# A graph layer on one core: another order for VectorE's instructions in the second round

## The reference

```python
h = jnp.maximum(_layernorm(x, axis=-1), 0.0)
hi_t = h @ W1_w[:HID] + dep_emb @ W1_w[HID:] + W1_b          # dep_emb = dep_emb_table[adj]
hj_t = h @ W2_w[:HID] + dep_emb @ W2_w[HID:] + W2_b
relevance = jnp.sum(hi_t * hj_t, axis=-1)
A = softmax(jnp.where(adj != 0, relevance, NEG), axis=2)
h_syn = relu((A @ h) @ gcn_w + gcn_b)
out = x + h_syn @ Wo_w + Wo_b
```

## Time and profile before

| | |
|---|---|
| median of three runs | 366.44 us (366.13 to 366.99) |
| the profiled execution | 366.79 us, span 364.9 us |
| PE busy | 354.9 us, 97% of the span |
| ACT busy | 272.9 us, 75% |
| DVE busy | 263.1 us, 72% |
| POOL busy | 178.8 us, 49% |
| granted TensorE clock | 1.00 throughout |
| the chain that ended last | PE 91%, DVE 5%, ACT 3%, issue 1% |

### The profile page before, as it was taken

One profiled execution on the slowest core, in us unless ns is written; L12 is line 12 of the kernel. 1 busy time (PEld: TensorE's weight loads), 2 busy tenths in 40 slices (PEclk: granted clock), 3 DMA queues, 4 the chain that ended last, 5 costly groups with the idle time before them and its releaser, 6 DMA issues.

```text
span 364.9 us, 9504 instructions
## 1 busy us (share of the span) xinstructions
PE 354.9 (97%) x3144; PEld 222.5 (61%) x3144; DVE 263.1 (72%) x667; ACT 272.9 (75%) x580; POOL 178.8 (49%) x348
## 2 busy tenths in 40 slices
PE   8999879999999999999999999999999999999986
PEld 8675546565756666565756666565756666565753
DVE  1788898595867777695867777695867777586664
ACT  3499586969698787879788787879788787865742
POOL 2046871573828284654728274654728274680000
PEclk9999999999999999999999999999999999999999
DMA  7962607764649484554649384564649364444052
GB/s 225 362 208 85 175 3 141 220 115 134 176 112 232 86 249 97 178 120 145 160 104 241 86 237 108 163 132 141 167 96 249 86 172 86 116 89 143 2 154 107
DMA packets 82215, 53.87 MB, mean 148 GB/s; under 512 B 45666, under 2 KB 82148, under 8 KB 82196
## 3 DMA queue, kind: packets, MB, share of 16 engines
q1 hardware_dynamic: 81488, 53.22, 55.8%
q0 software_dynamic: 64, 0.20, 0.3%
q10 hardware_dynamic: 644, 0.20, 0.3%
HBM read 17.44 MB, written 12.58 MB: 82 GB/s over the span
## 4 chain that ended last, share of the span: by engine, by line
PE 91%; DVE 5%; ACT 3%; issue 1%; DVEq 0%; POOL 0%; POOLq 0%
PE bank L1135 24%; PE bank L1136 24%; PE bank L1137 24%; PE bank L1233 5%; PE bank L1376 3%; PE bank L1371 3%; PE bank L1179 2%; PE bank L1147 2%; PE bank L1342 1%; PE bank L1170 1%; PE bank L1218 1%; PE bank L1441 1%; PE bank L1443 1%; DVE wo_lo L774 1%; DVE stats L683 1%
## 5 line engine op out<-in xcount | busy, mean ns | idle before, releaser
L422 POOL TENSOR_TENSOR h_parts<-h_tok,h_parts 128x1536 f16<-128x1536 f32 (+1 forms) x14 | 41.9, 2994 | 92.7 <-ACT h_parts L467 92.7
L1135 PE MATMUL bank<-gw_hi,hT 128*128 128x385 f16 x192 | 63.1, 329 | 1.9 <-DVE g_parts L867 1.6
L398 POOL TENSOR_TENSOR x_all<-x_all,bo_all 128x1536 f32 (+1 forms) x16 | 55.1, 3450 | 16.5 <-ACT h_tok L476 16.5
L1137 PE MATMUL bank<-gw_hi,hT 128*128 128x385 f16 x192 | 62.7, 327 | 0.0
L1136 PE MATMUL bank<-gw_lo,hT 128*128 128x385 f16 x192 | 62.6, 326 | 0.0
L1135 PE MATMUL bank<-wo_hi,z_hi 128*128 128x384 f16 x180 | 58.7, 326 | 0.0
L1136 PE MATMUL bank<-wo_lo,z_hi 128*128 128x384 f16 x180 | 58.7, 326 | 0.0
L1137 PE MATMUL bank<-wo_hi,z_lo 128*128 128x384 f16 x180 | 58.7, 326 | 0.0
L1135 PE MATMUL bank<-hT,m_hi 128*128 128x512 f16 x144 | 54.6, 379 | 0.5 <-DVE hT L697 0.5
L1136 PE MATMUL bank<-hT,m_hi 128*128 128x512 f16 x144 | 54.6, 379 | 0.0
L1137 PE MATMUL bank<-hT,m_lo 128*128 128x512 f16 x144 | 54.6, 379 | 0.0
(11 more groups left out here) (162 smaller groups left out, 691.9 us busy)
## 6 DMA issues: line engine op xcount, KB each, us to landing
x_all<-in_x_dram SPq DMA_DIRECT2D x16, 768.0 KB, 6.1
out_dram<-x_all SPq DMA_DIRECT2D x15, 768.0 KB, 4.0
hg_parts<-hg_lo SPq DMA_DIRECT2D x32, 192.0 KB, 3.3
hg_parts<-hg_hi SPq DMA_DIRECT2D x32, 192.0 KB, 3.6
x_all<-in_L_gnn_W_w_dram SPq DMA_DIRECT2D x2, 576.0 KB, 5.0
out_dram<-x_all SPq DMA_DIRECT2D x4, 192.0 KB, 1.9
gcn_raw<-in_L_gnn_gcn_w_dram SPq DMA_DIRECT2D x1, 576.0 KB, 10.8
x_all<-in_L_gnn_Wo_w_dram SPq DMA_DIRECT2D x1, 576.0 KB, 11.3
```

What stands on the lines that cost most here:

```text
L398: nc.gpsimd.tensor_tensor(x_all[:, s, :, :], x_all[:, s, :, :], bo_all[:, :, :].broadcast_to([P, KT, D]), ALU.add).then_inc(x_biased, 1)
L422: nc.gpsimd.tensor_tensor(h_parts[:, tiles, 1, :], h_tok[:, tiles, :], h_parts[:, tiles, 0, :], ALU.subtract).then_inc(h_split, 1)
L1135: nc.tensor.matmul(dst, lh, rh, start=(c == 0), stop=False)
L1137: last = nc.tensor.matmul(dst, ll, rh, start=False, stop=(c == DC - 1))
```

## The change

Three lists move, and no arithmetic changes.

DVE, before the jump of `typed`: the three `wo_low_part` are taken out of `second_round` and put behind the first `type_top`, behind `rows_and_low(0, 2)` and behind `rows_and_low(0, 3)`.

DVE, in `second_round`: `g_low_part(1, 0)` comes straight after `masked_scores(0)`; the statistics of x(3) are cut in two halves; `attention_high(1)` and the second half come ahead of `shared_high_parts(2)`; only the first half of the mask's bias is waited for at the start.

POOL: the second half of the mask's bias is made after `main_coefficients(2)` and no longer before it; `token_low(2)` comes before `main_coefficients(3)`.

```diff
@@ gpsimd
             make_bias(0)
+            main_coefficients(2)
             make_bias(1)
-            main_coefficients(2)
...
+            token_low(2)
             main_coefficients(3)
-            token_low(2)
@@ vector
-            def second_statistics(tiles):
+            def part_statistics(s, tiles):
+                if s == 1:
+                    dve.wait_ge(x1_loaded, 16)
+                    dve.wait_ge(coef_ready, COEF_STEPS)
+                else:
+                    dve.wait_ge(x_loaded, 16 * s)
+                    dve.wait_ge(coef_ready, COEF_STEPS * 2)
                 for k in tiles:
-                    ins = nc.vector.bn_stats(stats6[:, k, :], x_all[:, 1, k, :])
+                    ins = nc.vector.bn_stats(stats6[:, k, :], x_all[:, s, k, :])
...
+            wo_low_part(0)
             rows_and_low(0, 1)
...
             rows_and_low(0, 2)
+            wo_low_part(1)
             rows_and_low(0, DC)
+            wo_low_part(2)
...
             def second_round():
-                early_low_part(1, 0)
-                wo_low_part(0)
-                early_low_part(1, 1)
-                wo_low_part(1)
-                early_low_part(1, 2)
-                dve.wait_ge(bias_made, 2)
+                for c in range(DC):
+                    early_low_part(1, c)
+                dve.wait_ge(bias_made, 1)
                 masked_scores(0)
-                wo_low_part(2)
-                statistics(3)
+                g_low_part(1, 0)
+                part_statistics(3, range(0, 2))
+                attention(0, prev=False)
                 third_mean_made()
-                g_low_part(1, 0)
-                attention(0, prev=False)
                 g_low_part(1, 1)
+                attention_high(1, prev2=False)
+                part_statistics(3, range(2, KT))
                 shared_high_parts(2)
-                attention_high(1, prev2=False)
                 g_low_part(1, 2)
                 shared_low_parts(2)
+                dve.wait_ge(bias_made, 2)
                 aggregated(1)
```

More of the change, by code:

```diff
@@ L678, in statistics @@
                     dve.wait_ge(coef_ready, COEF_STEPS * s)
-                elif s in (1, 3):
-                    dve.wait_ge(coef_ready, COEF_STEPS * (s + 1) // 2)
                 for k in range(KT):
@@ L684, in statistics @@
                 ins.then_inc(stats_ready, 1)
-            def second_statistics(tiles):
-                dve.wait_ge(x1_loaded, 16)
-                dve.wait_ge(coef_ready, COEF_STEPS)
+            def part_statistics(s, tiles):
[5 more added lines that the diff above has]
+                    dve.wait_ge(coef_ready, COEF_STEPS * 2)
                 for k in tiles:
-                    ins = nc.vector.bn_stats(stats6[:, k, :], x_all[:, 1, k, :])
+                    ins = nc.vector.bn_stats(stats6[:, k, :], x_all[:, s, k, :])
                 if tiles[-1] == KT - 1:
@@ L835, in _ @@
                                     ALU.max).then_inc(scale_step, 1)
-            second_statistics(range(0, 1))
+            part_statistics(1, range(0, 1))
             peak_exponent(SC_WO, SC_GCN + 1, 5)
@@ L844, in _ @@
             scale_ready(SC_WO, SC_GCN + 1, 5, scale_step)
-            second_statistics(range(1, 2))
+            part_statistics(1, range(1, 2))
             dve.wait_ge(scale_step, 9)
@@ L848, in _ @@
                                     ALU.mult, ALU.mult).then_inc(weight_scales_ready, 1)
-            second_statistics(range(2, KT))
+            part_statistics(1, range(2, KT))
             nc.vector.tensor_scalar(out_half[:, :], unscale[:, SC_GCN:SC_GCN + 1], 1.0 / Y_SCALE, None,
```

## The result

The changed kernel takes 367.54 us (median of 11 runs, 366.51 to 368.47) against 366.44 us of the kernel before in the same session (11 runs, 366.06 to 367.13): ratio 1.0029, 95% interval 1.0017 to 1.0041. That is 1.1 us slower, where 0.6 was forecast. The profiled execution took 366.51 us, with a span of 364.7 us.

The account below looks back on a forecast made before the run. DVE's list was taken to bound the second round, the only stretch where PE stands still. Tile (1, 3) +0.68 and -0.10 behind it sum to +0.58 on 366.44, giving 367.0 us; range 365.2 to 367.6.

Parts of the forecast that it names:

- main case: Second round: POOL holds DVE at both places and the jump is hidden; 367.0 us, own range 366.6 to 367.4, chance 0.45.
- step 2: DVE before the jump: make_bias(0) on POOL holds wo_low_part(1) to 37.21; next row term at 37.74 instead of 36.91, +0.83.
- step 3: DVE at the jump: wo_low_part(2) at 38.35, early_low(1, 0) at 38.88 instead of 38.43, +0.45; jump taken as hidden.
- third rival: At the jump: register load comes only with the row term, early_low at 39.26, all 0.38 later; 367.4 us, chance 0.13.
- steps 4 to 6: DVE's middle: masks 40.70 (-0.74), reciprocal 45.35, PE's 1.37 us pause gone, attention_out 47.54, new wait for ACT some 0.5 us.
- step 7: POOL's token_low(2) holds DVE's shared_high second kind to 52.01; g_low(1, 2) at 52.67, PE's tile (1, 2) +0.4.
- step 8: End of the second round: z_lo at 54.34, hg_lo(1, 0) ends at 55.62, PE's tile (1, 3) at 55.68, +0.68 us.
- step 9: PE behind the second round: back to back; the 0.10 wait at 69.89 isn't met by a later PE, -0.10.
- check by terms: Cross-check of tile (1, 3)'s delay: gains of wo_lo and a pause against holds and waits, counted to +0.7 to +0.8.
- first rival: Second round: POOL doesn't hold DVE; 365.1 us with neither hold, 365.6 if only wo_low(1) is held; chance 0.25.
- second rival: At shared_high: DVE slips through, token_low holds shared_low instead; +0.16 - 0.10, 366.5 us, chance 0.12.
- fourth rival: PE's pause from 50.8 to 53.4: clock at half for the next 4 us of matmuls, up to 4, 371 us; chance 0.02.

Follow-up runs that it names:

- e5: The changed kernel once more, unaltered, in another session against the kernel before: 367.81 us, ratio 1.0032.
- e8: e2 with POOL's make_bias(0) moved ahead of main_coefficients(1): 367.06 us, ratio 1.0019 to the kernel before.
- e2: The changed kernel with POOL's token_low(2) also waiting until both shared low parts of DVE are done: 365.13 us, ratio 0.9958 to the kernel before.
- e9: The kernel before with POOL's new order alone and DVE's wait for the mask biases split as in the change: 367.36 us, ratio 1.0022.
- e6: The changed kernel with POOL's token_low(2) waiting for the four shared high parts, not the shared low parts: 366.51 us, ratio 0.9998 to the kernel before.
- e4: e2 with wo_low_part(1) moved behind rows_and_low(0, 3), next to wo_low_part(2): 365.03 us, ratio 0.9952 to the kernel before.
- e10: e2 with g_low(1, 2) ahead of the shared high parts, z_lo and hg_lo of chunk 0 ahead of the shared low parts: 365.44 us, ratio 0.9971.
- e11: e2 with Wo's three low parts left in the second round as in the kernel before: 365.91 us, ratio 0.9984 to the kernel before.
- e12: e6's wait, with DVE's g_low(1, 2), second statistics half, z and hg_lo of chunk 0 ahead of the shared low parts: 364.39 us, ratio 0.9948.
- e7: The kernel before with POOL's new order alone, DVE's single wait for both mask biases left as it was: 373.44 us, ratio 1.0184.

## Why the prediction was right, and where not

The sign and the mechanism held, and the main case was the one that came. That 367.54 lies in the range of 365.2 to 367.6, by 0.06 us, is partly luck: the range left out the clock, which was worth about 0.9 us here, and the 367.81 of e5, the same kernel in another session, would lie outside it.

- **The first hold (step 2).** Forecast: `wo_lo` of some 1.7 us at 36.1, the next row term at 37.74. Measured, on the old scale: 1.82 at 36.07, and 37.81. By the Trainium skill ("SBUF — State Buffer", Who interferes with whom) whoever issues first has the shared ports for its whole instruction. The traces agree, and e8's 1.76 us for two elements a partition shows how little the size of the held one matters.
- **The jump (step 3, third rival).** The load of the register in DVE's queue came at 36.2 in the new trace, within the held `wo_lo` (35.36 to 37.18), and `early_low` started at 38.93 (forecast 38.88, rival 39.26). The rival is out.

```profile
L253 DVEq TENSOR_LOAD <-has_types x1: 548/548/548, 36.2 to 36.2; - x1
```

- **DVE's middle (steps 4 to 6).** On the old scale the masks are at 40.73 (forecast 40.70), the reciprocal at 45.37 (45.35), ACT's `attention_out` at 47.56 (47.54), DVE's new wait for it 0.40 (0.5).
- **The second hold (step 7).** DVE's first instruction won the tie by 0.07 us, POOL got in between the two and held the other: `g_low(1, 2)` at 52.58 (52.67), PE at 53.32 (53.4) after a pause of 2.44 (2 to 3). e2 shows the price of this hold alone, 1.4 us, and e9 that of the one in DVE's old order, 0.8 us.
- **The term (steps 8 and 9).** Tile (1, 3) at 55.56 (55.68), which is +0.56 where step 8 had +0.68; up to the tile behind the round +0.46, so the -0.10 of step 9 came as forecast. PE waits nowhere from 57 us up to the last supertile. The check by terms at the end of step 8 was wrong: its figures give +0.85, and with the +0.45 that step 3 found for steps 2 and 3 together, in place of 0.83 + 0.14, +0.33. The forecast used the chain of starts, and not this check.
- **The two rivals with POOL.** Neither "POOL doesn't hold" nor "DVE slips through" came. Had nothing been held at the second place, the time would have been about 365.5 by e2's distance (366.44 - 0.95, an estimate), close to the 365.6 that the first rival has with one hold. The second rival had +0.06; e6, which brings it about, comes to about +0.36 (the estimate there).
- **What was mis-sized: the clock (fourth rival).** I saw the pause of 2 to 3 us and gave it a chance of 0.02 and up to 4 us. It came in 20 of 23 runs and costs 1.05 in the one trace that holds it; the 20 are on average 1.2 us slower than the three others. With it, 0.46 + 1.05 x 20/23 = 1.37; the two sessions measured 1.10 (0.6 to 1.5 by the interval) and 1.5 between the medians, 1.2 by the ratio. The clock held through 1.37 us before, and from that row nothing followed for 2.44 us; I should have carried this case as a term with a real chance.

Open: 0.3 us behind the last instruction. From the tile behind the second round to the start of DVE's last group PE and DVE need 290.21 to 290.24 us in all 14 traces. From there to the end of the span are 4.44 to 4.51 us in the seven kernels with an extra wait in `token_low` (e2, e4, e6, e8, e10, e11, e12) and 4.77 to 4.85 in the seven others. The group in after (span 364.7) and in e2 (span 363.2):

```profile
359.85 2.19 DVE L1001 SCALAR_TENSOR_TENSOR x_all<-bank,out_scale,x_all 128x384 f32<-128x384 f32 x4 [1.14 <-PE bank L1449]
...
358.73 2.19 DVE L1003 SCALAR_TENSOR_TENSOR x_all<-bank,out_scale,x_all 128x384 f32<-128x384 f32 x4 [1.13 <-PE bank L1451]
```

So 0.3 us of what those seven show against the kernel before, of e12's 2.0 too, is not the second round's. No run shows what makes it. Nor does any show why the clock didn't fall in three of the 23 runs.

## What to carry to other kernels

When an instruction is moved into a gap, look at what the neighbour engine does in that gap, and put beside a long POOL instruction only what POOL does not hold: here PSUM readers and bn_stats. Count the pauses of PE that a shorter list makes longer, not only their sum: one of 2.44 us cost another 1.05 in clock, where one of 1.37, and two of 1.2 and 1.7, cost none. And when part of a change is tried alone, carry over the waits that belong to it.

## What the runs showed of the hardware

- A held DVE instruction is recorded with the wait inside its length, and small ones are held too: 0.16 to 1.76 us for 128x2 (e8), as against 0.60 to 1.82 for 128x384 (after). In after, the reciprocal of 128x4 and two bn_stats beside POOL's second bias (43.77 to 45.67) kept their 0.18 and 1.01 us.
- POOL is held too: `token_low(2)` takes 1.85 us where it got in between two DVE instructions (after), 1.65 in the kernel before and in e12.
- DVE's queue passes on to a register load while an instruction ahead of it is held: the load at 36.2, `wo_lo` held from 35.36 to 37.18.
- After 2.44 us of standing PE went on at 2.4 GHz for 1.1 us and fell to 1.2 GHz only then, for 3.5 us (e5); in 3 of 23 runs of the same kernel it didn't fall. In e7, where PE stood 6.26 us, it fell before PE went on.
